# The last three images one by one, the final sum on VectorE, bfloat16 hits, more filler matmuls and a moved statistics stage in a one-core transformer block

## The reference, cut to what matters

```
h = layernorm(x) * (1 + ca) + sa
# attention: a soft sampling of 33 places per row, 8 heads of 16 channels
wave   = silu(h @ wave_w.T + wave_b);  freq, phase = means over heads of sigmoid/tanh of it
w      = silu(h @ kernel_w.T + kernel_b)[..., :33]
pos    = clip(base + s_idx * freq + phase, 0, 255);  g = linear interpolation of h at pos
x      = x + ga * silu(einsum(g, w) @ out_w.T)
# experts: 8 experts, the best 2 per row, hard mask
h      = layernorm(x) * (1 + cb) + sb
top2   = top_k(softmax(h @ router_w.T + router_b), 2);  mask = one_hot(top2).sum
x      = x + gb * (sum_e mask_e * (h @ expert_w_e.T + expert_b_e))
```

## Time and profile before

| what | value |
| --- | --- |
| device time, 3 runs | 308.44 us median, 308.04 to 310.49 |
| profiled execution | 310.25 us, span 308.4 us |
| PE busy | 270.5 us, 88% |
| DVE busy | 267.3 us, 87% |
| ACT busy | 232.6 us, 75% |
| POOL busy | 64.1 us, 21% |
| mean granted PE clock | 0.938 of full |

### The profile page before, as it was taken

How to read it: one execution, slowest core, us unless ns; L and a number is a source line. 1 busy time by engine, 2 the same in 40 slices (tenths; PEclk the granted TensorE clock), 3 DMA queues, 4 the chain that set the end, 5 groups by cost and what they waited for, 6 DMA issues and landing times.

```text
span 308.4 us, 5553 instructions
## 1 busy us (share of the span) xinstructions
PE 270.5 (88%) x1919; PEld 196.6 (64%) x1926; DVE 267.3 (87%) x555; ACT 232.6 (75%) x646; POOL 64.1 (21%) x59
## 2 busy tenths in 40 slices
PE   6680983999499999999999999999999999899995
PEld 2430732784388567875797579848784778577664
DVE  7979987999969789999999999979999999783462
ACT  4775778799967998799879988898679756754301
POOL 3103401620443010800280016202530200010100
PEclk9965767799959999999999999999999999999999
DMA  5630000020000400050005000320023002300101
GB/s 170 216 85 1 2 0 0 0 71 2 0 2 9 148 1 2 1 173 0 1 2 173 0 0 2 95 81 1 2 58 115 1 1 64 109 2 0 36 0 51
DMA packets 12011, 12.93 MB, mean 42 GB/s; under 512 B 1021, under 2 KB 10960, under 8 KB 11216
## 3 DMA queue, kind: packets, MB, share of 16 engines
q1 hardware_dynamic: 11540, 12.19, 13.4%
q10 hardware_dynamic: 444, 0.40, 0.5%
HBM read 10.44 MB, written 2.15 MB: 41 GB/s over the span
## 4 chain that ended last, share of the span: by engine, by line
PE 50%; ACT 18%; DVE 16%; issue 8%; DMA 5%; POOL 1%; ACTq 0%; DVEq 0%; POOLq 0%
PE pE L1134 9%; PE pT L1051 7%; PE pR L1051 6%; DVE AT L834 5%; PE pL L1110 5%; PE pR L1028 4%; ACT A L499 4%; DMA mkb<-mask_rows 3%; ACT xn L399 3%; PE pY L1065 3%; PE pY L1134 3%; PE pL L1102 2%; ACT c L482 2%; DVE hm L901 2%; PE pT L985 2%
## 5 line engine op out<-in xcount | busy, mean ns | idle before, releaser
L798 DVE COPY_PREDICATED T<-mask,T 128x672 f32<-128x672 int16 (+11 forms) x54 | 83.1, 1539 | 0.5
L834 DVE TENSOR_TENSOR AT<-T,c 128x2064 f32<-128x2064 f32 x32 | 72.4, 2305 | 0.0
L499 ACT ACTIVATE A<-pT 128x512 f32<-128x512 f32 x64 | 34.9, 596 | 23.7 <-PE pT L1051 23.5
L1134 PE MATMUL pE<-hm,late 128*128 128x256 f32 x224 | 52.6, 386 | 0.0
L1134 PEld LDWEIGHTS pE<-hm,late 128*128 128x128 f32 x224 | 41.2, 190 | 6.6
L1051 PE MATMUL pT<-first,AT 128*128 128x128 f32 x256 | 36.4, 289 | 9.2 <-DVE AT L844 9.2
L315 POOL TENSOR_SCALAR ve<-sq 128x4 f32<-128x4 f32 (+1 forms) x14 | 8.3, 590 | 173.8 <-ACT xn L365 173.8
L321 POOL TENSOR_TENSOR rs<-ve,mhalf 128x4 f32<-128x4 f32 (+1 forms) x18 | 32.9, 1827 | 46.6 <-DVE ve L711 39.8
L1051 PEld LDWEIGHTS pT<-first,AT 128*128 128x128 f32 x256 | 31.2, 150 | 15.2 <-DVE AT L844 10.8
L499 ACT ACTIVATE A<-pR 128x512 f32<-128x512 f32 x64 | 35.2, 610 | 1.0 <-PE pR L1051 1.0
L901 DVE TENSOR_TENSOR hm<-mkb,h2T 128x2048 f32<-128x2048 bf16 x13 | 29.8, 2289 | 6.5 <-DMA mkb<-mask_rows 6.5
(11 more groups left out here) (149 smaller groups left out, 418.8 us busy)
## 6 DMA issues: line engine op xcount, KB each, us to landing
mkb<-mask_rows SPq DMA_DIRECT2D x6, 1024.0 KB, 5.3
x<-in_x SPq DMA_DIRECT2D x7, 256.0 KB, 5.9
out<-x SPq DMA_DIRECT2D x7, 256.0 KB, 5.7
late<-in_late SPq DMA_DIRECT2D x1, 592.0 KB, 3.9
mkb<-mask_rows SPq DMA_DIRECT2D x1, 512.0 KB, 3.8
x<-in_x SPq DMA_DIRECT2D x2, 128.0 KB, 3.5
wmod<-in_wmod ACTq DMA_DIRECT2D x1, 256.0 KB, 4.1
out<-x SPq DMA_DIRECT2D x2, 128.0 KB, 3.5
```

The lines of the kernel that those rows point to most:

```text
L499: nc.scalar.activation(A[b][:, m, 2 * j:2 * j + 2, :].rearrange("p h l -> p (h l)"), four_banks(k)[:, :], ACT.Copy).then_inc(a_A, 1)
L798: nc.vector.copy_predicated(rows[:, :, :, j0:j1], spread(mask[:, k, 0:w, j0:j1], [P, w, H, j1 - j0], 2), rows[:, :, :, j0 + (1 << bit):j1 ...
L834: nc.vector.tensor_tensor(AT[:, bt, :, :].rearrange("p h (j r) -> p h j r", r=BLK), spread(T[n % 2][:, bt, 0:H, 0:NB], [P, H, NB, BLK], 3) ...
L1134: ins = mm(dst, weT[:, e, :], hm[b][:, e, :], start=False, stop=(e == E - 1))
```

## The change

Seven parts:

1. `UNITS`: image 0, six pairs (1,2) to (11,12), and then 13, 14 and 15 alone, so 10 units. `LATE` is image 14, `LAST` image 15, and the tail written by hand is shortened to match.
2. The last sum of every unit is on DVE (`total`, at the end of a step), with x read from SBUF. ACT's `total` and PE's product with the identity are gone.
3. `hit` is bfloat16 and is transposed against a bfloat16 identity that ACT makes once.
4. More fillers: 5 for 2 at the start, 18 for 9 in step -1, 38 new in step 0, 18 new in step 1, 12 new in step 2.
5. DVE: both `masked` inputs stand ahead of `residual`, the first one network stage earlier.
6. ACT: `stats2` stands behind `front_hs` and `sums1`.
7. `hm` buffers and their waits are generalised (`hm_of`, `hm_free`).

```diff
-UNITS = ((0, 1),) + tuple((i, 2) for i in range(1, B - 1, 2)) + ((B - 1, 1),)
+UNITS = ((0, 1),) + tuple((i, 2) for i in range(1, B - 3, 2)) + tuple((i, 1) for i in range(B - 3, B))
...
-        hit = sb("hit", [P, BT, 2, NP * E]);
+        hit = sb("hit", [P, BT, 2, NP * E], BF16); ident16 = sb("ident16", [P, P], BF16);
...
+        def hm_of(n, b):
+            return hm[b if n < LATE else (n - LATE + 1) % 2]
+
+        def hm_free(n, b):
+            last = [before(m) + q for m in range(n) for q in range(UNITS[m][1]) if hm_of(m, q) is hm_of(n, b)]
+            return last[-1] + 1 if last else 0
...
             def store(n):
-                if n < LATE - 1:
-                    sp.wait_ge(a_out, n + 1)
-                else:
-                    sp.wait_ge(v_out, n - LATE + 2)
+                sp.wait_ge(v_out, n + 1)
...
-            def total(n):
-                act.wait_ge(t_out, n + 1)
-                nc.scalar.activation(of_x(n), moe_bank(n)[:, 0:tiles(n) * C].rearrange("p (a c) -> p a c", c=C),
-                                     ACT.Copy).then_inc(a_out, 1)
...
                 run(i, 1, front_wave)
                 if i == -1:
                     clear(3)
-                run(i, -1, stats2)
+                    act.wait_ge(d_first, 16)
+                    nc.scalar.activation(ident16[:, :], ident, ACT.Copy).then_inc(a_id, 1)
                 if i >= 0:
                     run(i, 1, front_hs)
                 run(i, 2, sums1)
+                run(i, -1, stats2)
                 run(i, 1, front_u)
...
-                run(i, -2, total)
...
-            mid_A(LATE, 1)
...
+            back_moe(LATE - 1)
             mid_A(LAST, 0)
...
@@ vector, main loop
-                run(i, 0, network, range(2, 4))
+                run(i, 0, network, range(2, 3))
                 run(i, -2, masked, 0)
+                run(i, 0, network, range(3, 4))
+                second(i, -2, masked, 1)
                 run(i, 0, network, range(4, 5))
                 run(i, -1, residual)
-                second(i, -2, masked, 1)
...
                 second(i, 0, set_ends, 1)
+                run(i, -2, total)
...
@@ vector, tail
-            masked(LATE - 1, 1)
             residual(LATE)
...
             masked(LATE, 0)
             total(LATE - 1)
-            masked(LATE, 1, range(0, 2))
             route(LAST)
-            masked(LATE, 1, range(2, 4))
...
@@ tensor
-            warm_up(2)
+            warm_up(5)
...
-                        ins = mm(pL[0:NP * E, bt * P:(bt + 1) * P], hit[:, bt, k, :], ident,
+                        ins = mm(pL[0:NP * E, bt * P:(bt + 1) * P], hit[:, bt, k, :], ident16[:, :],
...
             def back_out(n):
                 pe.wait_ge(a_moe, before(n + 1))
                 for bt in range(tiles(n)):
-                    dst = moe_bank(n)[:, bt * P:(bt + 1) * P]
-                    if n < LATE - 1:
-
-                        pe.wait_ge(v_x2, n + 1)
-                        mm(dst, ident, of_x(n)[:, bt, :], start=True, stop=False)
-                        ins = mm(dst, moeT[:, bt * P:(bt + 1) * P], ident, start=False, stop=True)
-                    else:
-                        ins = nc.tensor.transpose(dst, moeT[:, bt * P:(bt + 1) * P], ident)
+                    ins = nc.tensor.transpose(moe_bank(n)[:, bt * P:(bt + 1) * P], moeT[:, bt * P:(bt + 1) * P], ident)
...
                 if i == -1:
-                    warm_up(9)
+                    warm_up(18)
                 run(i, -2, back_experts, 0)
                 second(i, -2, back_experts, 1)
+
+                if i == 1:
+                    warm_up(18)
+                elif i == 2:
+                    warm_up(12, pT[0])
                 run(i, -1, back_x2T)
                 if i > 0:
                     warm_up(4, pT[0])
                 run(i, -1, back_logits)
-                if i > 0:
+
+                if i == 0:
+                    warm_up(38)
+                elif i > 0:
                     warm_up(2, pT[0])
```

More of the change, by code:

```diff
@@ L607, in _ @@
             back_mk(LATE)
-            back_moe(LATE - 1)
             norm2(LAST)
             back_h2T(LAST)
+            back_moe(LATE)
             back_mk(LAST)
-            back_moe(LATE)
             back_moe(LAST)
@@ L887, in masked @@
                 dve.wait_ge(a_h2T, before(n) + b + 1)
-                if n > 0:
-                    dve.wait_ge(t_moe, before(n - 1) + min(b, UNITS[n - 1][1] - 1) + 1)
+                if hm_free(n, b) > 0:
+                    dve.wait_ge(t_moe, hm_free(n, b))
                 own = h2T_of(n)[:, b * L:(b + 1) * L]
@@ L900, in masked @@
                     dve.wait_ge(d_mkb[n % 2], 16 * (n // 2 + 1))
-                nc.vector.tensor_tensor(hm[b][:, :, :], mkb[n % 2][:, :, b * L:(b + 1) * L],
+                nc.vector.tensor_tensor(hm_of(n, b)[:, :, :], mkb[n % 2][:, :, b * L:(b + 1) * L],
                                         spread(own, [P, E, L], 1), ALU.mult).then_inc(v_hm, 1)
@@ L907, in total @@
                 nc.vector.tensor_tensor(of_x(n), moe_bank(n)[:, 0:tiles(n) * C].rearrange("p (a c) -> p a c", c=C),
-                                        of_x(n), ALU.add).then_inc(v_out, 1)
+                                        of_x(n),
+                                        ALU.add).then_inc(v_out, 1)
             start()
@@ L1133, in back_experts @@
                         pe.wait_ge(v_hm, masked_before(img) + e // 2 + 1)
-                    ins = mm(dst, weT[:, e, :], hm[b][:, e, :], start=False, stop=(e == E - 1))
+                    ins = mm(dst, weT[:, e, :], hm_of(n, b)[:, e, :], start=False, stop=(e == E - 1))
                 if own[-1] == E - 1:
@@ L1195, in _ @@
                 run(i, 0, mid_attend, 0, 1)
-            mid_A(LATE, 1, 0)
-            mid_A(LATE, 1, 1)
-            mid_attend(LATE, 1, 0)
-            mid_attend(LATE, 1, 1)
             mid_y(LATE)
-            back_experts(LATE - 1, 0)
+            back_experts(LATE - 1, 0, range(0, 4))
             mid_gate(LATE)
+            back_experts(LATE - 1, 0, range(4, E))
             mid_A(LAST, 0, 0)
```

33 lines of the change are left out of this document (13 added, 20 removed).

## The result

The changed kernel takes 327.86 us in the median of 4 runs (326.19 to 329.12), the kernel before beside it 308.24 (304.91 to 310.49): a ratio of 1.064 [1.058, 1.070]. The forecast was 317.4. The direction was right and the size was not: 19.6 us lost for 9.0.

What follows compares the result with a forecast made beforehand. DVE was taken to bound the kernel, busy 31.0 of a 32.2 us pair step. Steps up to the residual of image 14 (293.1) plus a tail of 24.3 gave 317.4 us; own range 312 to 322, outer 304 to 328.

Steps and rivals of the forecast that it cites:

- 55.4 ... 90.8: Bias rows of steps 1 and 2, POOL held behind DVE's AT pair: 55.4 us (56.77 before) and 90.8 (88.50).
- A DVE idle of about 7 us for `mkb` in step 8: Sign to look for: in step 8 DVE reaches the masked input at mark + 5.5 and waits to 12.9, 7.4 us.
- step 7: Network of one image reaches the masked input at mark + 10.5, masks at 12.9: 2.4 us wait, 28.15 in all.
- Three early waits: DVE's waits in the front, shrunk by early fillers to about 0.7 together: 4.8 us earlier at unit 2's line.
- From there the chain is shorter by one image ... 24.3 for 34.6: Tail from the residual of image 14 to the end: 24.3 us for 34.6, uncertain from 22 to 27.
- bf16 hits and no identity product: room, not time: PE in pair steps: 0.9 us less identity products, hits 0.65 for 1.75, `mkT` 2.0 us earlier; room, not time.
- Never held: Rival: POOL's operation finishes by the pair or takes the ports, DVE yielding under 1 us: 304.6 us, chance 0.2.
- Held in nearly every step: Rival: POOL held in steps 3 to 6 too, 4.4 to 5.3 us each: 322 to 333 us, chance 0.2.
- Costs cancel: Rival: masks reach step 8 sooner, 3 us less, and some holds end between AT products: 307 to 311.5, chance 0.17.
- the terms of step 8: DVE's wait, masked inputs, network stages, line, products and AT in the second single-unit step, given as 27.8 us.

Runs made afterwards that it cites:

- e1: The changed kernel with the units and tail of the kernel before (pairs up to 13,14), all else changed: 306.32 us, ratio 0.988.
- e2: The changed kernel with stats2 back in its old place, ahead of hs and sums1: 318.35 us, ratio 1.032.
- e9: The kernel before with fillers, bfloat16 hits and the change's single units and tail; sum, masked inputs, stats2 as before: 316.27 us, ratio 1.022.
- e6: The kernel before with the fillers and bfloat16 hits alone: 294.66 us, ratio 0.953.
- e12: e7 with the logits of image 15 ahead of the last two experts of 14, and fillers before its mask product and copies: 327.51 us, ratio 1.056.
- e7: The changed kernel with fillers added in PE's idle times of the tail: 325.34 us, ratio 1.052.
- e4: The kernel before with the changed kernel's fillers alone: 302.17 us, ratio 0.980.
- e10: e6 with the last sum on DVE, masked inputs in their old places: 295.64 us, ratio 0.956.
- e5: The kernel before with fillers, bfloat16 hits, sum on DVE and masked inputs earlier; stats2, units and tail as before: 298.84 us, ratio 0.966.
- e11: e6 with `near` and the next unit's first network stage ahead of the second AT pair on DVE: 299.62 us, ratio 0.967.
- e3: The changed kernel with DVE waiting for POOL's `nm` ahead of the AT pair in steps 1 and 2: median 326.07 us, 318.75 to 329.35.

## Why the prediction was wrong

**The steps: right.** The change was to bring the last residual 19.3 us later than before (293.1 for 273.77); it came 18.1 later (291.91), and against e1, which differs in the units alone, 19.8 later. "55.4 ... 90.8": `rs` and `nm` of steps 1 and 2 were held as costed, 8.3 us by step 2 in e2 against the change. "A DVE idle of about 7 us for `mkb` in step 8": 6.50. In step 7 3.95 for 2.4. Three early waits of 1.93, 1.43 and 2.10 became 0.29, none and 0.21, with the line of unit 2 at 43.34 for a forecast 43.65. Steps of pairs took 31.36 for 31.6, 0.24 less than I gave, and DVE was busy 31.15 of them.

**The step that failed: "From there the chain is shorter by one image ... 24.3 for 34.6".** I took the tail before as work of three images and subtracted 10.3 us for one. It is a chain of latencies that image 13 had mostly lain beside. Taking it out saved 0.1 us at the clock the tail got (e9 against e6: 32.6 and 32.7), and 3.8 at full clock with the old order of PE (e12 against e6 and e1: 28.9 and 32.7). Even there the logits of image 15 come no sooner, 16.3 us behind the residual for 16.5 in e6 (276.96 less 260.48); the 3.8 are saved behind them. Mark by mark behind the residual of image 14 (us):

| | forecast | after | e12 |
| --- | --- | --- | --- |
| logits of 14 | 8 | 9.4 | 8.1 |
| masked inputs of 14 begin | 11 | 14.4 | 12.7 |
| logits of 15 | 15.2 | 21.7 | 16.3 |
| masked inputs of 15 begin | 17.5 | 24.8 | 20.7 |
| last sum | 22.1 | 30.4 | 26.3 |
| end | 24.3 | 33.0 | 28.9 |

Of the 8.7 us, 4.1 are given back by fillers and the order of PE (e12): PE's half clock from 302.0 to 312.2, which I had not put in, made the masks and the first four experts of image 14 slow, and the logits of 15 stood behind all eight. e7 against the change puts 2.8 of it on the fillers, though its last experts ran partly at half clock (5.41 us for 3.72 for the sixteen products). The other 4.6 are the chain itself: 1.1 up to the logits of 15, 2.1 more up to its masked inputs (PE is still at experts of 14 and their output), 1.0 more to the last sum, 0.4 behind it. The first 1.4 us come from image 13: its experts at half clock kept the transposes of A to 293.43, 1.5 us behind the residual, where e12 has them 0.2 behind (296.56). In both, `norm2` of image 14 stands on ACT behind eight evacuations of A (to 298.0 in the changed kernel, though `nm` was there at 294.60); with pairs these evacuations begin 1.3 us ahead of the residual (259.19 and 260.48 in e6), which is one reason why the tail with image 13 in it takes so little longer.

**"bf16 hits and no identity product: room, not time": wrong for the hits alone.** They gained 7.5 us with pairs (e4 to e6). My own rows had the two waits of DVE that they removed, and `rs` held, 0.35 ahead of the pair. Freeing `rs` was the smaller part: e6 gained 1.3 us in the step where it passed, and 0.4 in the next, where it was held as in e4. In the sum this hid, since the steps were costed from DVE's floor, where the hits' gain is already in. The eight products start within 0.40 us at full clock (118.76 to 119.16 in e6, 57 ns from each to the next), so the lower end, 0.45, was right. The Trainium skill's page "TensorE: Matmul & The Clock Gate", Back-to-back issue gap, has 81 ns for such a stream, which is above what this trace shows.

**Prices of the parts, from the medians of the runs.** Each row adds one edit to the row above.

| kernel | us | ratio |
| --- | --- | --- |
| before | 308.2 to 309.5 | 1 |
| + fillers (e4) | 302.17 | 0.980 |
| + bfloat16 hits (e6) | 294.66 | 0.953 |
| + sum on DVE (e10) | 295.64 | 0.956 |
| + masked inputs earlier (e5) | 298.84 | 0.966 |
| + stats2 moved (e1) | 306.32 | 0.988 |
| + single units and their tail (the change) | 327.86 | 1.064 |

Fillers were forecast at 4.8 and gave 6 to 7. The sum was forecast at 0.6 a step and cost 1.0 in all; the masked inputs were forecast at nothing and cost 2.3 to 3.2; the units were forecast at 9 us or so (19.3 later up to the last residual, less 10.3 in the tail) and cost 21.5. Rounds differ by 1 us in the kernel before, so these prices hold to 1 or 2 us. Only the units and stats2 were priced in more than one place: 19.5, 21.5 and 21.6 (e9), 7.5 and 9.5.

**The rivals.** "Never held" is out: steps 1 and 2 were held. "Held in nearly every step" gave 322 to 333 and the time lies there, but by luck, through another mechanism: in steps 3 to 5 `rs` passed (147.45, 1.01 us). Its margin of the forecast, 0.35, was in fact 1.42: DVE took up the line at 145.84, 23.4 behind the mark, as forecast (23.6), but `ve` came 1.1 us sooner, at 147.16 for 25.8 behind the mark. "Costs cancel" is out. Two of my sums are off by roundings that change nothing: the terms of step 8 add up to 27.65 for 27.8, those of "never held" to 304.85 for 304.6.

**The rule on ports.** In these traces, e11 apart, an `rs` of a pair of images (`128x4`) that begins 0.58 us or more ahead of an AT pair isn't held to its end (1.01 us, at most 1.4), and one that begins 0.33 to 0.55 ahead is (5.99 to 6.20 us, 17 of 17 rows); one that begins 0.02 ahead gets through at the gap between the two products (3.18 in e3, as in the 2.87 us of 46.36 above). In e11 `near` or a network stage in front did the holding. The Trainium skill, "SBUF — State Buffer", SBUF: two separate sides, gives the ports to whichever starts first. The mutual exclusion agrees; the order agrees only from a lead of 0.58 us on. Why that much lead is needed stays open.
